# Two pairs' first maxima inside the 3x3 convolution's last tile, late queries' low half on GpSimd, and a group-norm variance one stage later

## The reference

```python
t = cbs(x, cv1_w, cv1_bn, 0)
ys = [t[:, :C], t[:, C:]]
for i in range(N):
    yi = ys[-1]
    z = cbs(yi, m_cv1_w[i], m_cv1_bn[i], 1)           # 3x3 convolution, 256 -> 256 channels
    z = bot_attention(z, m_qkv_w[i], m_rw[i], m_rh[i])
    z = jax.nn.silu(bn_eval(conv2d(z, m_cv2_w[i], 0), m_cv2_bn[i]))
    ys.append(yi + z)
return cbs(jnp.concatenate(ys, axis=1), cv2_w, cv2_bn, 0)
# bot_attention: 4 heads of 64, 1024 positions
logits = jnp.einsum('bhdi,bhdj->bhij', q, k + r) * HD ** (-0.5)
a = jax.nn.softmax(logits, axis=-1)
out = jnp.einsum('bhij,bhdj->bhdi', a, v)
```

## Time and profile before

| | us |
|---|---|
| median of 3 runs (lowest, highest) | 3345.95 (3345.1, 3348.13) |
| the profiled execution | 3342.8 |
| its span, first to last instruction | 3340.9 |
| TensorE busy in it | 3074.9 (92%) |
| VectorE busy | 1874.0 (56%) |
| ScalarE busy | 1571.2 (47%) |
| GpSimd busy | 1048.8 (31%) |
| mean granted TensorE clock | 0.979 |

### The profile page before, as it was taken

One profiled execution on the slowest core, in us unless ns is written; L12 is line 12 of the kernel. 1 busy time (PEld: TensorE's weight loads), 2 busy tenths in 40 slices (PEclk: granted clock), 3 DMA queues, 4 the chain that ended last, 5 costly groups with the idle time before them and its releaser, 6 DMA issues.

```text
span 3340.9 us, 61223 instructions
## 1 busy us (share of the span) xinstructions
PE 3074.9 (92%) x27308; PEld 1576.5 (47%) x27308; DVE 1874.0 (56%) x2515; ACT 1571.2 (47%) x1826; POOL 1048.8 (31%) x768
## 2 busy tenths in 40 slices
PE   3779989999999999999999999999999999998997
PEld 3534544444544545445444445445454454444453
DVE  5536465474655656464654746546564646537463
ACT  1315465172732646254651727326462556517272
POOL 1113451052511443134411525114431344115051
PEclk8889999999999999999999999999999999999998
DMA  4200000200011000100002000110001000010001
GB/s 140 77 26 29 1 30 26 79 2 29 11 45 51 2 29 24 54 29 1 30 26 77 4 29 8 41 58 2 29 23 54 30 1 30 26 46 10 1 8 44
DMA packets 35894, 105.60 MB, mean 32 GB/s; under 512 B 12976, under 2 KB 15024, under 8 KB 32944
## 3 DMA queue, kind: packets, MB, share of 16 engines
q1 hardware_dynamic: 35632, 101.69, 8.5%
HBM read 80.18 MB, written 21.50 MB: 30 GB/s over the span
## 4 chain that ended last, share of the span: by engine, by line
PE 78%; DVE 9%; ACT 6%; issue 4%; POOL 2%; SPq 0%; DMA 0%; POOLq 0%; DVEq 0%
PE ps_u L678 50%; PE ps_u L837 12%; DVE row_max L1198 4%; PE ps_o L859 4%; ACT wide L985 3%; PE ps_o L860 3%; PE ps_o L861 3%; PE ps_u L811 3%; PE ps_u L697 2%; ACT ps_u L985 1%; POOL y_pad L1306 1%; DVE qk L1187 1%; POOL z L1306 1%; PE ps_u L869 1%; ACT qk L967 1%
## 5 line engine op out<-in xcount | busy, mean ns | idle before, releaser
L678 PE MATMUL ps_u<-y_pad,w_c 128*128 128x512 f16 x3456 | 781.8, 383 | 0.0
L1198 DVE TENSOR_REDUCE row_max<-ps_u 128x2 f32<-128x1024 f32 x512 | 618.3, 1221 | 195.3 <-PE ps_u L811 195.3
L1332 POOL TENSOR_TENSOR probs<-wide,probs 128x1024 f16<-128x1024 f32 x256 | 545.4, 2130 | 540.3 <-ACT probs L989 529.6
L678 PEld LDWEIGHTS ps_u<-y_pad,w_c 128*128 128x128 f16 x3456 | 329.8, 97 | 419.2 <-issue 14.5
L1006 DVE SCALAR_TENSOR_TENSOR wide<-wide 128x512 f32<-128x512 f32 x256 | 182.8, 716 | 610.9 <-ACT wide L905 609.0
L904 ACT ACTIVATE wide<-ps_u,par_m_t 128x512 f32<-128x512 f32 x128 | 99.4, 777 | 815.0 <-PE ps_u L678 815.0
L837 PE MATMUL ps_u<-qk 64*128 64x512 f16 x3072 | 420.0, 379 | 47.5 <-ACT shift_rows L977 19.6
L859 PEld LDWEIGHTS ps_o<-v_ext,probs 128*128 128x128 f16 x4096 | 375.7, 96 | 143.5 <-issue 129.0
L859 PE MATMUL ps_o<-v_ext,probs 128*128 128x65 f16 x4096 | 431.3, 193 | 0.0
L860 PE MATMUL ps_o<-v_ext,probs 128*128 128x64 f16 x4096 | 429.1, 195 | 0.0
L861 PE MATMUL ps_o<-v_ext,probs 128*128 128x65 f16 x4096 | 426.5, 191 | 0.0
(11 more groups left out here) (182 smaller groups left out, 3951.5 us busy)
## 6 DMA issues: line engine op xcount, KB each, us to landing
w_c<-w_c_dram SPq DMA_DIRECT2D x15, 2304.0 KB, 8.7
xn<-in_x_dram SPq DMA_DIRECT2D x32, 512.0 KB, 5.9
o_nat<-in_x_dram SPq DMA_DIRECT2D x64, 256.0 KB, 2.6
out_dram<-qk SPq DMA_DIRECT2D x32, 512.0 KB, 2.7
w_c_dram<-w_c SPq DMA_DIRECT2D x2, 2304.0 KB, 7.9
qk<-in_L_conv_m_cv_w_dram SPq DMA_DIRECT2D x2, 1152.0 KB, 7.1
probs<-in_L_conv_m_cv_w_dram SPq DMA_DIRECT2D x2, 1152.0 KB, 10.8
probs<-in_L_conv_cv_w_dram SPq DMA_DIRECT2D x2, 1024.0 KB, 11.9
```

What stands on the lines that cost most here:

```text
L678: ins = e.matmul(o, lhsT, rhs, start=start and k == 0, stop=stop and k == len(pairs) - 1)
L1198: e.reduce_max(row_max[:, g % 2, :, it, half], ps_u[:, use.slot:use.slot + 2, :], axis=AX.X).then_inc(*dve_max.up(i, b, g, half, it))
L1332: e.tensor_tensor(p_part(s, 1), wide[:, w.slot, :], p_part(s, 0), ALU.subtract).then_inc(*pool_lo.up("p", i, b, s))
```

## The change

1. `order[1:3] = order[2:0:-1]` in `plan_maxima`: the maxima of groups 0 and 1 no longer come as group 0 in full and then group 1. Now both groups' maxima over the first key half come first (max 0,0,x and max 1,0,x), then group 0's over the second half, then group 1's. `shift` of a group stands behind its second half.
2. q(1,0) and k(1,0) move into `conv_begin(1,1)`, behind its second quarter. A max 1,0,0 stands ahead of `conv_end(1,1)`, a max 1,0,1 behind it, and v0, v1, v2, v3 lie between the further maxima. 16 maxima are made by the fourth logits step, where there were 15.
3. q(0,1) and q(1,1) (`ON_POOL`): ScalarE now makes two passes over the PSUM tile, a float32 copy into a `wide` buffer and the cast, and GpSimd subtracts. VectorE does nothing for them. The bank is free when ScalarE is done. The logits that read them (steps 16 and later) wait for GpSimd's semaphore.
4. q(0,1) stands ahead of `shift_row` of group 0, and no v or max stands between that and the first logits.
5. `gn_var` moves from behind `conv_end(1,1)` of b = 0 to behind `conv_end(0,0)` of b = 1; there two norm steps now stand behind `conv_end(1,0)` (one before).

```diff
-        NORM_PARTS = {(0, 0, 0): 1, (0, 0, 1): 0, (0, 1, 0): 1, (0, 1, 1): 1, (1, 0, 0): 2, (1, 0, 1): 1, (1, 1, 0): 1, (1, 1, 1): 0}
-        HALF_0 = (("q", 1, 0), ("k", 1, 0), ("v", 0), ("v", 1))
+        NORM_PARTS = {(0, 0, 0): 1, (0, 0, 1): 0, (0, 1, 0): 1, (0, 1, 1): 0, (1, 0, 0): 2, (1, 0, 1): 2, (1, 1, 0): 1, (1, 1, 1): 0}
+        BESIDE = ((), (("q", 1, 0), ("k", 1, 0)), (), ())
...
+        ON_POOL = ("q", 0, 1), ("q", 1, 1)
...
+            order = [(g, half) for g in range(len(GROUPS_OF)) for half in range(2)]
+            order[1:3] = order[2:0:-1]
...
+                w, freed_by = None, ("dve_lo", key)
+                if (kind, *at) in ON_POOL:
+                    w, freed_by = wide_ring.take(("pool_lo", key)), ("act_cast", key)
...
-            for _ in plan_conv_begin(i, b, 1, 1):
+            for _, beside in zip(plan_conv_begin(i, b, 1, 1), BESIDE):
                 next(maxima)
+                for at in beside:
+                    piece(*at)
+            next(maxima)
             conv_end(1, 1)
+            next(maxima)
...
+                    if w:
+                        until_free(e, w)
+                        e.activation(wide[:, w.slot, 0:HALF], ps_u[:, use.slot, :], ACT.Copy, scale=qkv_unit[:, b, m:m + 1])
...
+                elif kind == "project":
+                    what, i, b, pair, n, use, w = a
+                    if w:
+                        e.wait_ge(*act_cast.at(what, i, b, pair, n))
+                        dst = (q_parts, k_parts)[what == "k"]
+                        e.tensor_tensor(dst[:, 1, pair, HH[n]], wide[:, w.slot, 0:HALF], dst[:, 0, pair, HH[n]],
+                                        ALU.subtract).then_inc(*pool_lo.up(what, i, b, pair, n))
```

More of the change, by code:

```diff
@@ L403, in plan_maxima @@
         def plan_maxima(i, b):
-            for g, (n, pair) in enumerate(GROUPS_OF):
-                for half in range(2):
-                    for it in range(4):
-                        key = (i, b, g, half, it)
-                        plan("max", *key, banks.take(0.25, 1.6, ("dve_max", key), pair=True))
-                        yield
-                plan("shift", i, b, g)
+            order = [(g, half) for g in range(len(GROUPS_OF)) for half in range(2)]
+            order[1:3] = order[2:0:-1]
+            for g, half in order:
+                for it in range(4):
+                    key = (i, b, g, half, it)
+                    plan("max", *key, banks.take(0.25, 1.6, ("dve_max", key), pair=True))
+                    yield
+                if half:
+                    plan("shift", i, b, g)
         def plan_shift_row(i, b, g):
@@ L435, in piece @@
                 key = (kind, i, b, *at)
-                if kind == "v":
-                    plan(*key, banks.take(1.3, 1.6, ("dve_lo", key)))
-                else:
-                    plan("project", *key, banks.take(2.6, 1.6, ("dve_lo", key)))
+                w, freed_by = None, ("dve_lo", key)
+                if (kind, *at) in ON_POOL:
+                    w, freed_by = wide_ring.take(("pool_lo", key)), ("act_cast", key)
+                plan(*(() if kind == "v" else ("project",)), *key, banks.take(1.3 if kind == "v" else 2.6, 1.6, freed_by), w)
             def conv_end(m, n):
@@ L463, in plan_bottleneck @@
                     next(maxima)
+                if at == ("v", 3):
+                    next(maxima)
             plan_shift_row(i, b, 0)
-            piece("v", 3)
-            next(maxima)
             o_uses, threads = {}, []
@@ L484, in plan_bottleneck @@
                     plan_av(s - LAG)
-                next(maxima, None)
-                if s == 3:
-                    next(maxima)
+                if s > 0:
+                    next(maxima, None)
                 w = None
@@ L783, in tensor @@
                 elif kind == "project":
-                    what, i, b, pair, n, use = a
+                    what, i, b, pair, n, use, w = a
                     m = pair + (HT if what == "k" else 0)
@@ L826, in tensor @@
                     n, pair = GROUPS_OF[g]
-                    once(dve_lo, "q", i, b, pair, n)
+                    once(pool_lo if ("q", pair, n) in ON_POOL else dve_lo, "q", i, b, pair, n)
                     once(dve_lo, "k", i, b, pair, jt // 4)
@@ L842, in tensor @@
                     n, pair = GROUPS_OF[g]
-                    once(dve_lo, "v", i, b, jt // 2)
+                    once(pool_lo if ("v", jt // 2) in ON_POOL else dve_lo, "v", i, b, jt // 2)
                     if way(s)[1] == "vector":
@@ L969, in scalar @@
                 elif kind == "v":
-                    i, b, jj, use = a
+                    i, b, jj, use, w = a
                     e.wait_ge(*u_full.at("v", i, b, jj))
+                    if w:
+                        until_free(e, w)
+                        e.activation(wide[:, w.slot, 0:HALF], ps_u[:, use.slot, :], ACT.Copy, scale=V_SHIFT)
                     e.activation(v_tile(jj)[:, :, 0:HD], ps_u[:, use.slot, :].rearrange("p (a d) -> p a d", d=HD), ACT.Copy,
@@ L1178, in vector @@
                 elif kind == "project":
-                    what, i, b, pair, n, use = a
+                    what, i, b, pair, n, use, w = a
                     key = (what, i, b, pair, n)
                     m = pair + (HT if what == "k" else 0)
+                    if w:
+                        continue
                     e.wait_ge(*act_cast.at(*key))
@@ L1332, in gpsimd @@
                     e.tensor_tensor(p_part(s, 1), wide[:, w.slot, :], p_part(s, 0), ALU.subtract).then_inc(*pool_lo.up("p", i, b, s))
+                elif kind == "project":
+                    what, i, b, pair, n, use, w = a
+                    if w:
+                        e.wait_ge(*act_cast.at(what, i, b, pair, n))
+                        dst = (q_parts, k_parts)[what == "k"]
+                        e.tensor_tensor(dst[:, 1, pair, HH[n]], wide[:, w.slot, 0:HALF], dst[:, 0, pair, HH[n]],
+                                        ALU.subtract).then_inc(*pool_lo.up(what, i, b, pair, n))
+                elif kind == "v":
+                    i, b, jj, use, w = a
+                    if w:
+                        ve = v_tile(jj)
+                        e.wait_ge(*act_cast.at("v", i, b, jj))
+                        e.tensor_tensor(ve[:, :, HD + 1:2 * HD + 1], wide[:, w.slot, 0:HALF].rearrange("p (a d) -> p a d", d=HD),
+                                        ve[:, :, 0:HD], ALU.subtract).then_inc(*pool_lo.up("v", i, b, jj))
                 elif kind == "m2_split":
```

6 lines of the change are left out of this document (2 added, 4 removed).

## The result

The changed kernel takes **3330.43 us** (3328.38 to 3331.15, 5 runs) against 3345.95 (3345.1 to 3348.13, 5 runs) of the kernel before: a ratio of 0.9951, 95% interval 0.9938 to 0.9964.

What follows compares the result with a forecast made beforehand. TensorE, busy 92% of 3340.9 us, bounds the kernel; only its gaps and clock losses can be won. +6.5 + 2.8 - 13.3 = -4.0, so 3345.95 - 4.0 = 3342.0 us; range 3333 to 3353.

Steps and rivals of the forecast that it cites:

- the walk from the first logits to the zeros: Head of attention, from logits at 18.15 to zeros at 26.14 us; 1.20 of the gain of 2.56 lies here.
- later groups: Attention groups after the first: maxima per step unchanged, shift-row wait stays, no TensorE gaps worth naming: 0, +-2 bank turns.
- from first max to zeros, undisturbed: Head plus the projections moved ahead of it: 29.17 us against 28.70 (0.47 more) or 28.84 (0.33 more), summing to +6.5.
- waits in b = 1: TensorE's second max in b = 1 comes 0.4 us late, bounds 0 and 1.2; seven images: +2.8, bounds 0 and +8.4.
- clock in the heads: TensorE's clock fall, seen in twelve of 16 heads, taken as gone: -13.3 us; the other end is 0.
- the variance, where it arrives: gn_var was taken off the heads of b = 0; no TensorE cost was booked for its new place in b = 1.
- The walk to the first logits: Head from the end of conv_end(1,1): shift 16.06, shift_row 16.28, first logits 18.15 us against 19.51 before, gaining 1.36.
- The shift comes no earlier: In the head, shift starts 16.06 us after the end of conv_end(1,1), against 15.95 before.
- the queue on ScalarE: In the head, q(0,1)'s two passes stand ahead of the shift's copy on ScalarE, costing 0.5 us.
- Rival 2: Unknown costs at their low ends (ScalarE's extra pass 0.60, GpSimd never late in b = 1): 3333.8 us, faster; chance 0.32.
- The sixteenth max: One more max ahead of the end of conv_end(1,1), put at 0.22 us of TensorE's time.

Runs made afterwards that it cites:

- the slices: Changed kernel with conv_end(1,1) cut into 6, 4, 4 and 4 matmuls and a max in each cut: 3323.6 us, ratio 0.993.

## Why the prediction was wrong

The forecast was -4.0 us on the profiled execution; -11.65 came (3342.8 to 3331.15). Two steps failed: the walk from the first logits to the zeros was 0.27 us too long in each head (4.4 us), and the later groups were put at 0 where they give 3.6 us. Step by step, for all bottlenecks:

| step | forecast | measured |
|---|---|---|
| from first max to zeros, undisturbed | +6.5 | +2.1 (9 x 0.19 + 7 x 0.05) |
| waits in b = 1 | +2.8 (7 x 0.4) | +1.8 (7 x 0.26) |
| clock in the heads | -13.3 | -13.3 |
| later groups | 0 | -3.6 (16 times 0.22 to 0.23) |
| the variance, where it arrives | 0 | +1.0 (7 x 0.14) |
| ahead of the first max of all | 0 | +1.4 (256.97 against 255.62) |
| behind the last group's first zeros | 0 | -0.7 (103.46 against 104.16) |
| sum | -4.0 | -11.3, of the -11.5 between the spans |

The last two steps are no work of the change. Up to the first max all the kernels here issue the same work, and it starts between 254.43 and 257.43 in them; the stretch at the end, which no edit here touches, takes 102.85 to 104.27.

- **The walk to the first logits was right.** shift was put at 16.06 and came at 16.13 from the end of the convolution (2367.27, 0.09 ahead of the first max), shift_row was put at 16.28 and came at 16.36, the logits at 18.15, as forecast. "The shift comes no earlier" held, and so did the queue on ScalarE. That the logits fit to 0.01 is luck: q(0,1)'s two passes began 0.17 later than forecast (16.35 for 16.18) and took 0.17 less (1.15 for 1.32).
- **From there to the zeros it was 0.27 us too long**: the two passes over q(1,1) were put at 1.39, with 4.29 ahead of them; they took 1.24 (1.30 up to the start of the max behind them, at 2391.95) and 4.15 (2386.50 to 2390.65). Another 0.06 is a slip in the sum: 24.90, one max of 0.22 and the logits' 0.96 make 26.08, not 26.14. The float32 pass was taken from L905 (0.77) as the nearest kind; it measures 0.67 to 0.69, though, and the second pass starts 0.57 behind it. Sixteen times 0.27 is 4.4 us, the largest mis-sized term. The Trainium skill ("ScalarE: Activation LUTs", section "What ACT_TABLE_LOAD costs") says that ACTIVATE instructions right behind each other overlap by about 93 ns; the trace agrees (0.67 listed, 0.57 apart). Rival 2 had named this ("the unknown costs are at their low ends"), with 0.34 a head, and it came nearest to what happened; its other half, a GpSimd that is never late in b = 1, did not come.
- **"In the later groups ... 0" was wrong in kind, not only in size.** The sixteenth max (0.22) was counted as a cost ahead of conv_end and again nowhere as a gain. But a max that is made early is one that the third group no longer makes: 0.22 there and 0.22 back. A moved instruction has to be booked at both ends; this one was booked at one. Worth 3.6 us. `gn_var` is the same slip the other way round: the walk took its 0.14 us off seven heads of b = 0 and put nothing where it arrives, +1.0 us.
- **b = 1** waited 0.26 rather than 0.4, within its bounds.
- **The clock** came out as taken: -13.3. The sixteen heads of after are all at 1.00, with gaps of 1.36, 0.83, 1.38 and 0.95 us. The Trainium skill ("TensorE: Matmul & The Clock Gate", section "A second HAM failure mode: psum-queue depth-cycling") warns that many small idles between groups cycling through PSUM can swing the clock; the heads of after have just such idles and show no fall. But the margin is thin: without GpSimd's low parts the same order had falls again, and so had four heads with the other order of maxima.
- **The profiled execution of before lay 3.15 us below its median, and that of after 0.7 above.** So of the 15.5 us between the medians 3.9 are no part of any stretch that the traces show. Their cause is open. They decide on which side of the range's low end the time falls: the change of the profiled execution, taken off the median of before, gives 3334.3, inside it.

**What was luck.** The forecast booked GpSimd's part and the new order in one walk, and that walk was near the truth, but the near-zero it gave was two large terms: on the order before, GpSimd's part alone is worth 19 us, and the new order costs, on top of that, some 21 us undisturbed (18.1, 1.8 for the waits and 1.0 for the variance), of which it won 12.7 back by the clock. The prediction weighed the change as a whole only. Nothing in it would have told that the new order is better left out.

## What to carry to other kernels

Cost each part of a change on the kernel without the others as well, since a sum near zero may be two large terms, one of which can be had alone. Before work is moved out of a stretch, ask which engine is late there and what the moved work costs on the engine that is full in the place it goes to: here 3.02 us of TensorE's time were moved from where it idled to where it never did, and the slices did the same with three maxima. And book every moved instruction twice, where it arrives and where it leaves.
